# A graph kernel in fp32 on one core: the heads of two attention layers are set end to end

## The reference

```python
def gat_conv(x, src, dst, W, a_src, a_dst, bias, H, C, n):
    h = (x @ W).reshape(n, H, C)
    s_src = (h * a_src).sum(-1)
    s_dst = (h * a_dst).sum(-1)
    e = leaky_relu(s_src[src] + s_dst[dst], 0.2)
    ee = exp(e - segment_max(e, dst)[dst])
    alpha = ee / segment_sum(ee, dst)[dst]
    return segment_sum(alpha[:, :, None] * h[src], dst).reshape(n, H * C) + bias
out1 = gat_conv(layer_norm(x), ..., W1, a_src1, a_dst1, b1, 4, 192, N)
out2 = gat_conv(out1, ..., W2, a_src2, a_dst2, b2, 2, 96, N)
x = layernorm(x + concat([x, out2]) @ Wu + bu)
# then a relational graph layer: 34 relations, each a 768x768 weight, and a GCN
```

## Time and profile before

| | |
|---|---|
| median of 3 runs | 3441.8 us (3441.11 to 3443.11) |
| the profiled execution | 3440.49 us, of which the span is 3438.6 us |
| busy in the span | PE 93%, DVE 66%, ACT 42%, POOL 48% |
| gat1, first mask step to PE's end | from 554.58 us to 716.45 us |
| gat2, first mask step to PE's end | from 795.01 us to 859.94 us |
| one chunk of gat2 on PE, ten matmuls of 97 columns | 2.42 us |
| turning `out2` (L2101), start | 862.87 us, after an idle time of 2.94 us |
| the four weight maxima behind gat2's normalise (L1577) | 5.13 us from 862.85 us |
| loads of `xu_dram` behind gat2's normalise | 4.4 us from issue to landing |
| load of Wux issued, and PE's first work on x tiles (L1986) | 205.69 us and 453.23 us |
| weights of the first relation, issued | 784.91 us |

### The profile page before, as it was taken

How to read it: one execution, slowest core, us unless ns; L and a number is a source line. 1 busy time by engine, 2 the same in 40 slices (tenths; PEclk the granted TensorE clock), 3 DMA queues, 4 the chain that set the end, 5 groups by cost and what they waited for, 6 DMA issues and landing times. The chain is left out here.

```text
span 3438.6 us, 59477 instructions
## 1 busy us (share of the span) xinstructions
PE 3187.5 (93%) x17127; PEld 1997.9 (58%) x17127; DVE 2263.9 (66%) x4636; ACT 1452.8 (42%) x2678; POOL 1636.4 (48%) x1373
## 2 busy tenths in 40 slices
PE   6989988887589999999999999999999998879998
PEld 4544457886345555555555666666666664435545
DVE  8989997758844454554544878888888774533324
ACT  3767745636333333333343546555554632000100
POOL 3730000000346657666632665666666635777771
PEclk9999998998789999999999999999999999989999
DMA  3020012011243333333333555646555545675551
GB/s 97 2 74 0 0 54 82 1 45 43 94 123 109 126 126 109 126 117 119 126 108 131 178 185 174 203 160 199 177 181 178 175 148 158 185 227 157 159 128 52
DMA packets 230649, 415.83 MB, mean 121 GB/s; under 512 B 37108, under 2 KB 179955, under 8 KB 230566
## 3 DMA queue, kind: packets, MB, share of 16 engines
q1 hardware_dynamic: 169696, 272.25, 23.0%
q0 software_dynamic: 60480, 142.01, 15.5%
q10 hardware_dynamic: 390, 0.50, 0.1%
HBM read 263.22 MB, written 151.32 MB: 121 GB/s over the span
## 5 line engine op out<-in xcount | busy, mean ns | idle before, releaser
L2174 PE MATMUL bank<-arena 128*128 128x384 f16 x3675 | 1202.0, 327 | 22.0 <-DVE arena L1718 11.6
L2176 PE MATMUL bank<-arena 128*128 128x384 f16 x3675 | 1200.7, 327 | 0.0
L2177 PE MATMUL bank<-arena 128*128 128x384 f16 x3675 | 1200.5, 327 | 0.0
L1143 ACT ACTIVATE arena<-bank,winv 128x384 f32<-128x384 f32 x700 | 401.1, 578 | 878.4 <-PE bank L2177 861.8
L1718 DVE SCALAR_TENSOR_TENSOR arena<-bank,winv,arena 128x384 f32<-128x384 f32 x525 | 316.7, 613 | 412.5 <-PE bank L2177 411.4
L2174 PEld LDWEIGHTS bank<-arena 128*128 128x128 f16 x3675 | 360.1, 98 | 275.3 <-DVE arena L1718 17.2
L2177 PEld LDWEIGHTS bank<-arena 128*128 128x128 f16 x3675 | 360.1, 98 | 238.8 <-issue 2.0
L2176 PEld LDWEIGHTS bank<-arena 128*128 128x128 f16 x3675 | 360.5, 98 | 233.3 <-issue 6.5
L749 POOL DMA_INDIRECT arena<-y_half,idx_now x360 | 400.6, 1113 | 172.7 <-issue 101.8
L1611 DVE SCALAR_TENSOR_TENSOR arena<-arena,wscale 128x1152 f16<-128x1152 f32 x245 | 366.5, 1530 | 169.9 <-ACT arena L1054 162.0
L736 POOL DMA_INDIRECT w_now<-rel_inv_dram,idx_now x360 | 341.1, 947 | 253.9 <-ACT idx_now L1128 153.1
(11 more groups left out here) (245 smaller groups left out, 4136.3 us busy)
## 6 DMA issues: line engine op xcount, KB each, us to landing
y_half<-arena SPq DMA_DIRECT2D x306, 384.0 KB
arena<-in_L_gnn_W_rel_dram SPq DMA_DIRECT2D x68, 1152.0 KB, 5.9
arena<-y_half,idx_now POOLq DMA_INDIRECT x720, 3.2
y_half<-arena SPq DMA_DIRECT2D x34, 294.0 KB
w_now<-rel_inv_dram,idx_now POOLq DMA_INDIRECT x360, 2.6
cT_dram<-arena SPq DMA_DIRECT2D x1, 5625.0 KB
arena<-cT_dram SPq DMA_DIRECT2D x9, 625.0 KB
arena<-in_x_dram SPq DMA_DIRECT2D x10, 384.0 KB, 11.1
```

Source lines behind the costliest of these rows:

```text
L1143: nc.scalar.activation(y[half][:, :, c * CQ:(c + 1) * CQ], acc, ACT.Copy, scale=scale).then_inc(r_copied, 1)
L2174: nc.tensor.matmul(acc, h, w_hi[m - 1][:, k, :], start=fresh and k == 0, stop=False, skip_group_check=True)
L2176: nc.tensor.matmul(acc, h, w_lo[m - 1][:, k, :], start=False, stop=False, skip_group_check=True)
L2177: ins = nc.tensor.matmul(acc, l, w_hi[m - 1][:, k, :], start=False, stop=k == KH - 1, skip_group_check=True)
```

## The change

The change touches both attention layers and nothing else:

- Next head's rows: PE turns `zz` after chunk 1 and `lmax` after chunk 4. ScalarE copies `zz` after its Exp of chunk 4 into the other of two tiles (`bcL`, `unused`), and `lmax` into `bc1` after that of chunk 8. `leaky` and `minus` run one chunk ahead across the head boundary too.
- First head: its `zz` row goes to banks 2 to 4, right behind the `lmax` row, and VectorE copies it out. cT tile 8 is turned ahead of the rows, tile 9 behind them. A one-column Exp on ScalarE stands ahead of its row copy.
- Sums: PE's last chunk of a head signals after each bank, and normalise waits bank by bank. Its product is one broadcast multiplication per bank (and one more for the 98-row tile), without the bias.
- Biases: `b1` and `b2` are loaded as columns, element by element, and ScalarE adds them while it copies the turned `out1` and `out2`. The two loads that broadcast them to 128 partitions are gone.
- `out1` and `out2` are turned as soon as the banks that a group needs are normalised.
- The W2 step moves from behind gat1 into VectorE's program of heads 1 and 2, one pair in each of chunks 2 to 7.

```diff
-prod2 = unused[:, 0:D2]
+prod2 = view(vecV + 8 * D2, [D2])
...
-b2row = view(vecV + 8 * D2, [D2])
+b2col = bcol[:, 0:H2]
...
+  def summed(g, i):
+    h, c = divmod(i, NT)
+    return h * (NT - 1 + g.banks) + (NT - 1 + g.banks if c == NT - 1 else c + 1)
+  def bank_summed(g, h, k):
+    return h * (NT - 1 + g.banks) + NT + k
...
+O1_BANKS = (5, 6, 7, 0, 1, 2)
+def out_needed(g, k):
+  last = cdiv(NBANKS[g][1], P) - 1
+  here = O1_BANKS[k] + 1 if O1_BANKS[k] < gat1.banks else 0
+  return max(last // gat1.per + 1, here)
...
+gat2 = Gat("gat2", H2, C2, s2, s2_ready, h2, out2)
+O2_BANK = gat2.banks
...
-    ("x", range(4, 6)), ("row", 3), ("x", range(6, X_FIRST)), ("cT", range(CT_EARLY, CT_WAITS)),
-    ("row", H1), ("row", H1 + 1), ("cT", range(CT_WAITS, NT))]
+    ("x", range(4, 6)), ("row", 3), ("x", range(6, X_FIRST)), ("cT", range(CT_EARLY, NT - 1)),
+    ("row", H1), ("row", H1 + 1), ("cT", range(NT - 1, NT))]
+CT_LAST = (NT - 1) * len(NBANKS)
+def cT_bank(i):
+  return bank[i % 5 if i < CT_LAST else (0, 1, 5)[i - CT_LAST]]
...
-  sp.dma_start(row_a[:, :], b1.partition_broadcast(P)).then_inc(row_loaded, 16)
...
   sp.wait_ge(h_ready, NT * HALVES)
+  with nc.allow_non_contiguous_dma(reason="short vectors, a few hundred elements"):
+    sp.dma_start(gcol[:, :], col(b1)).then_inc(row_loaded, 16)
...
+  with nc.allow_non_contiguous_dma(reason="short vectors, a few hundred elements"):
+    sp.dma_start(b2col[0:C2, :], b2.rearrange("(j c) -> c j", c=C2)).then_inc(a2_loaded, 16)
   def keep_xu(n):
...
+        nc.scalar.copy(cT[0:rows(c), c, a:b], cT_bank(i)[0:rows(c), 0:b - a]).then_inc(cT_ready, 1)
...
-    else:
+    elif which == H1:
+      nc.scalar.activation(credit[:, 3:4], ones[:, 0:1], ACT.Exp)
       act.wait_ge(gat1.max, NT * H1)
-      spread_copy(gat1, which, (bc1, bcL)[which - H1])
+      spread_copy(gat1, H1, bc1)
...
-        act.wait_ge(g.pv, i - 3)
+        act.wait_ge(g.pv, g.summed(i - 4))
       nc.scalar.activation(ring[i % 4][0:r, :], bc1[0:r, :], ACT.Identity,
                 bias=mx[0:r, c, h:h + 1]).then_inc(g.lk, 1)
     if g is not gat1:
...
-      row(g.H + 1, bcL)
     act.wait_ge(g.shift, 2)
...
-      if c + 1 < NT:
+      if i + 1 < g.H * NT:
         leaky(i + 1)
       r = rows(c)
       act.wait_ge(g.t, i + 1)
       nc.scalar.activation(ring[i % 4][0:r, :], ring[i % 4][0:r, :], ACT.Exp).then_inc(g.ex, 1)
+      if h + 1 < g.H and c == 4:
+        row(g.H + 2 * h + 2, (bcL, unused)[(h + 1) % 2])
       if h + 1 < g.H and c == NT - 2:
         act.wait_ge(g.lk, NT * (h + 1))
-        row(g.H + 2 * h + 2, bc1)
-      if h + 1 < g.H and c == NT - 1:
-        leaky(i + 1)
-        act.wait_ge(g.t, NT * (h + 1))
-        row(g.H + 2 * h + 3, bcL)
+        row(g.H + 2 * h + 3, bc1)
   gat(gat1)
+  act.wait_ge(row_loaded, 16)
...
-      nc.scalar.copy(o1T[:, k, a:b], bank[i % 6][:, 0:b - a]).then_inc(o1T_ready, 1)
+      nc.scalar.activation(o1T[:, k, a:b], bank[O1_BANKS[k]][:, 0:b - a], ACT.Identity,
+                bias=gcol[:, k:k + 1]).then_inc(o1T_ready, 1)
   nc.scalar.copy(h2.rearrange("p n h c -> p (n h) c")[:, :, C2], ones[:, 0:NT * H2]).then_inc(h_ones, 1)
   for n in range(NT):
...
-      nc.scalar.copy(o2T[0:C2, j, a:b], bank[i][0:C2, 0:b - a]).then_inc(o2T_ready, 1)
+      nc.scalar.activation(o2T[0:C2, j, a:b], bank[O2_BANK + i][0:C2, 0:b - a], ACT.Identity,
+                bias=b2col[0:C2, j:j + 1]).then_inc(o2T_ready, 1)
...
-    dve.wait_ge(g.shift, 2)
+    dve.wait_ge(g.bc_psum, g.H + 2)
+    for j, (a, b) in enumerate(NBANKS):
+      ins = nc.vector.tensor_copy(bcL[:, a:b], bank[2 + j][:, 0:b - a])
+    ins.then_inc(g.shift, 1)
+    dve.wait_ge(g.shift, 3)
     def minus(i):
       h, c = divmod(i, NT)
       r = rows(c)
-      if c == 0:
-        dve.wait_ge(g.bc, g.H + 2 * h + 2)
+      if c == 0 and h:
+        dve.wait_ge(g.bc, g.H + 2 * h)
...
+      nc.vector.scalar_tensor_tensor(ring[i % 4][0:r, :], (bcL, unused)[h % 2][0:r, :], g.s[0:r, c, h:h + 1],
                      ring[i % 4][0:r, :], ALU.add, ALU.max).then_inc(g.t, 1)
     def normalise(h):
-      dve.wait_ge(g.pv, NT * (h + 1))
       for k in range(g.banks):
+        dve.wait_ge(g.pv, g.bank_summed(h, k))
...
+        at = slice(h * g.C, (h + 1) * g.C)
+        num = bank[k][:, 0:g.per * (g.C + 1)].rearrange("p (a c) -> p a c", c=g.C + 1)[:, 0:len(full), 0:g.C]
+        ins = nc.vector.tensor_tensor(
+          g.res[:, full[0]:full[-1] + 1, at], num,
+          rden[:, full[0]:full[-1] + 1].unsqueeze(2).broadcast_to([P, len(full), g.C]), ALU.mult)
         for b in tiles:
-          r = rows(b)
-          at = slice(h * g.C, (h + 1) * g.C)
-          ins = nc.vector.scalar_tensor_tensor(g.res[0:r, b, at], g.acc(b, r, 0, g.C), rden[0:r, b:b + 1],
-                            g.brow[0:r, at], ALU.mult, ALU.add)
+          if b not in full:
+            r = rows(b)
+            ins = nc.vector.tensor_scalar(g.res[0:r, b, at], g.acc(b, r, 0, g.C), rden[0:r, b:b + 1],
+                           None, ALU.mult)
         ins.then_inc(g.out, 1)
...
-      if (i + 1) % NT:
+      if i + 1 < g.H * NT:
         minus(i + 1)
...
-        minus(i + 1)
+      if g is gat1 and h in (1, 2) and 2 <= c < 2 + KT:
+        w2_vectors((h - 1) * KT + c - 2)
...
+  def w2_vectors(i):
+    k, j = divmod(i, 2)
+    if i == 0:
+      dve.wait_ge(w2_loaded, 16)
+      dve.wait_ge(a2_loaded, 48)
+    after(nc.vector.tensor_tensor(prod2, W2s[:, k, 0:D2], (a2s, a2d)[j], ALU.mult))
+    ins = nc.vector.tensor_reduce(W2s[:, k, D2 + j * H2:D2 + (j + 1) * H2],
+                   prod2.rearrange("p (h c) -> p h c", h=H2), AX.X, ALU.add)
+    after(ins)
+    if i == 2 * KT - 1:
+      nc.vector.memset(credit[:, 2:3], 0.0).then_inc(w2a_ready, 1)
   dve.wait_ge(mask_ready, NT)
...
   gat(gat1)
-  dve.wait_ge(w2_loaded, 16)
-  dve.wait_ge(a2_loaded, 48)
-  dve.wait_ge(gat1.pv, NT * H1)
-  for k in range(KT):
-    for j, a in enumerate((a2s, a2d)):
-      after(nc.vector.tensor_tensor(prod2, W2s[:, k, 0:D2], a, ALU.mult))
-      after(nc.vector.tensor_reduce(W2s[:, k, D2 + j * H2:D2 + (j + 1) * H2],
-                     prod2.rearrange("p (h c) -> p h c", h=H2), AX.X, ALU.add))
-  nc.vector.memset(credit[:, 2:3], 0.0).then_inc(w2a_ready, 1)
...
     if done == g.H:
       pe.wait_ge(g.shift, 1)
-    if done:
-      pe.wait_ge(g.bc, done)
+    if done == g.H + 1:
+      if g is gat1:
+        pe.wait_ge(cT_ready, CT_LAST)
+      else:
+        pe.wait_ge(xu_copied, HALVES * NT)
+    elif done:
+      pe.wait_ge(g.bc, done if done <= g.H else done - 1)
     g.turned[0] = done + 1
     h, k = divmod(done - g.H, 2)
-    column = g.s[:, :, done] if done < g.H else (lmax, zz)[k][:, :, h]
+    column = g.s[:, :, done] if done < g.H else ((zz, lmax) if h else (lmax, zz))[k][:, :, h]
+    first = 2 if done == g.H + 1 else 5
     for n in range(NT):
...
       at = n * P % BANK
-      ins = nc.tensor.transpose(bank[5 + n * P // BANK][:, at:at + r],
+      ins = nc.tensor.transpose(bank[first + n * P // BANK][:, at:at + r],
...
-        if i >= cs[0] * len(NBANKS) + 5:
+        if cs[0] * len(NBANKS) + 5 <= i < CT_LAST:
           pe.wait_ge(cT_ready, i - 4)
+        if i == CT_LAST + 2:
+          pe.wait_ge(gat1.bc, H1 + 1)
...
           r = rows(n)
-          ins = nc.tensor.transpose(bank[i % 5][0:rows(c), n * P - a:n * P - a + r],
+          ins = nc.tensor.transpose(cT_bank(i)[0:rows(c), n * P - a:n * P - a + r],
                        counts[0:r, n, c * P:c * P + rows(c)], ident[0:r, 0:r])
...
-    pe.wait_ge(cT_ready, len(NBANKS) * (cs[-1] + 1))
+    if cs[-1] != NT - 2:
+      pe.wait_ge(cT_ready, len(NBANKS) * (cs[-1] + 1))
...
           ins = nc.tensor.matmul(g.acc(b, r), ring[(h * NT + c) % 4][0:rc, b * P:b * P + r],
                      g.h[0:rc, c, h, :], start=(c == 0 and b % g.per == 0),
                      stop=(c == NT - 1), skip_group_check=True)
-        ins.then_inc(g.pv, 1)
-        if c in (NT - 3, NT - 2) and h + 1 < g.H:
+          if c == NT - 1 and (b % g.per == g.per - 1 or b == NT - 1):
+            ins.then_inc(g.pv, 1)
+        if c < NT - 1:
+          ins.then_inc(g.pv, 1)
+        if c in (1, 4) and h + 1 < g.H:
           row()
...
   for g, (a, b) in enumerate(NBANKS):
...
         pe.wait_ge(o1T_ready, i - 5)
+      pe.wait_ge(gat1.out, (H1 - 1) * gat1.banks + out_needed(g, k))
...
-        ins = nc.tensor.transpose(bank[i % 6][:, n * P - a:n * P - a + r], out1[0:r, n, k * P:(k + 1) * P],
+        ins = nc.tensor.transpose(bank[O1_BANKS[k]][:, n * P - a:n * P - a + r], out1[0:r, n, k * P:(k + 1) * P],
...
-  pe.wait_ge(gat2.out, H2 * gat2.banks)
-  pe.wait_ge(gat2.bc, 3 * H2)
+  pe.wait_ge(gat2.bc, 3 * H2 - 1)
...
+      pe.wait_ge(gat2.out, j * gat2.banks + (cdiv(b, P) - 1) // gat2.per + 1)
...
-        ins = nc.tensor.transpose(bank[i][0:C2, n * P - a:n * P - a + r], out2[0:r, n, j * C2:(j + 1) * C2],
```

(1 more changed line is left out.)

16 lines of the change are left out of this document (6 added, 10 removed).

## The result

The changed kernel takes 3405.68 us (median of 4 runs, 3403.84 to 3407.63); the kernel before, in the same comparison, 3442.45 (4 runs, 3441.11 to 3444.12). The ratio is 0.9895, interval 0.9883 to 0.9906: 36.8 us less, where 40.2 were predicted. The profiled execution took 3403.84 us (span 3402.0, mean clock 0.977), 36.65 less than that of before, and is used for the sum.

The account below looks back on a forecast made before the run. PE was taken to set the pace inside a head, with time lost at head boundaries and layer starts and ends. Six terms summed to 40.2 us, 3440.5 to 3400.3, given as 3401.5 for the median; range 3394 to 3413.

Parts of the forecast that it names:

- A: Start of gat1: first mask step at 549.15 instead of 554.58, 5.4 us gained, bounds 4 and 6.5.
- B: gat1's three head boundaries: VectorE's 2.2 us lead and normalise of 3.6 us gain 16.1 us, bounds 11 and 19.
- C: From gat1 to h2: turning takes 9.7 us with ScalarE's 18 copies as chain, 4.5 us gained, bounds 3 and 6.
- D: Start of gat2: first mask step at 791.45 instead of 795.01, 3.5 us gained, bounds 2.5 and 4.5.
- E: Inside gat2, bound by VectorE: mask steps run 56.5 us instead of 61.7, 5.2 us gained, bounds 3.5 and 5.5.
- F: End of gat2: PE's end to first addition takes 7.2 us instead of 12.7, 5.5 gained, bounds 2.5 and 6.
- Rival 1: Heads 1 and 2 of gat1: VectorE becomes the bound through chunks with W2 pairs; 3408, chance 0.11.
- Rival 2: Ahead of x tile 3: the element load of b2 delays it by up to 6.5 us; 3408, chance 0.05.
- Rival 3: Boundaries, C and F: TensorE's clock falls after remaining waits, 2 to 2.6 us each; 3412, chance 0.06.
- The stretch behind it should keep its length: Behind the first addition, expected near 832.5 after gat2: the changed profile would show no change in length.
- Rival 4: gat1's chunks: the clock stays low through them, 2.6 us a chunk, slower than before, up to 3505; chance 0.03.
- Rival 5: Behind 872.65: an unmoved transfer or weight load makes something wait and gives the gain back; 3441, chance 0.03.

Follow-up runs that it names:

- e5: The changed kernel itself, unchanged, run again; 3405.06 us beside 3443.21 for the kernel before, ratio 0.9889.
- e12: The changed kernel itself, unchanged, run a third time; 3583.69 us beside 3621.14 for the kernel before, ratio 0.9894.
- e2: The changed kernel, but normalise waits ahead of every bank for the signal of the head's last bank; 3600.48 us, ratio 0.9930 to the kernel before.
- e3: The changed kernel with the division tile by tile, ten products for a head instead of one for each bank; 3672.48 us, ratio 1.0124 to the kernel before.
- e8: The changed kernel with late rows (turned at chunks 7 and 8, lmax first) and the old boundary order; 3425.51 us, ratio 0.9945 to the kernel before.
- e9: The changed kernel with late rows alone (turned at chunks 7 and 8), new boundary order kept; 3618.45 us, ratio 0.9988 to the kernel before.
- e1: The changed kernel with the next head's first leaky and minus back behind the last chunk's Exp and mask step; 3587.43 us, ratio 0.9891.
- e4: The changed kernel with W2's twelve pairs back behind gat1's last normalise; 3587.95 us, ratio 0.9895 to the kernel before.
- e7: The changed kernel with every second of the 18 copies of turned features done by VectorE instead of ScalarE; 3401.36 us, ratio 0.9879.
- e10: The changed kernel with copies of turned features shared by ScalarE and VectorE, unread transposes in TensorE's waits, column products with a scalar operand; 3578.07 us, ratio 0.9876.
- e6: The changed kernel with TensorE's short waits filled by transposes that nobody reads; 3401.86 us beside 3405.06 for the changed kernel.
- e11: The changed kernel with the division tile by tile, the same kernel as e3 run once more; 3663.54 us, ratio 1.0122 to the kernel before.

## Why the prediction held, and where it was off

In us, by the prediction's own terms, from the table (after, with e5 and e12 in brackets):

| term | predicted | measured |
|---|---|---|
| A, start of gat1 | 5.4 | 5.55 (4.49, 4.04) |
| B, boundaries | 16.1 | 16.27 (15.70, 15.95) |
| C, gat1 to h2 | 4.5 | 4.54 (4.55, 4.53) |
| h2 product | none | -1.68 (-0.02, -1.69) |
| D, to gat2 | 3.5 | 2.14 (3.58, 3.57) |
| E, inside gat2 | 5.2 | 5.99 (5.86, 5.35) |
| F, to the first addition | 5.5 | 6.14 (6.14, 5.28) |
| to the relations | none | -1.88 (-1.93, -0.05) |
| behind them | none | -0.47 |
| sum | 40.2 | 36.6 |

The six terms with a mechanism sum to 40.6, in e5 and e12 to 40.3 and 38.7. That the first is within 0.5 of 40.2 is luck in part: D fell short by 1.4, E and F went over by 0.8 and 0.6. The rest of the loss is in stretches that the prediction left as they were. (The last step of the sum, 3400.3 and 1.3, gives 3401.6 and not 3401.5.)

- A and D were right in their steps: the copy of `zz` by VectorE, the table load ahead. From the start of the `lmax` row to gat1's first mask step are 14.55 us before, 8.91 after and in e12, and 9.63 in e5, so 5.6, 5.6 and 4.9; the rest of the difference in the table lies ahead of that row, which starts between 539.7 and 542.4 in these profiles. D's 2.14 comes from both spread rows at 1.2 GHz; the other two profiles have 3.58 and 3.57.
- B rested on VectorE's lead of 2.2 us and a normalise of 3.6. e2 measured the lead as a wait of 2.2; normalise took 3.64 in the changed kernel, and e3 shows that its length passes through. From TensorE's end of head 0 (587.90) to its end of gat1 (694.63) are 106.7 us, as predicted; 0.2 of the table's 16.27 lie in head 0. What the prediction had not separated is which part carries the gain: it takes the early place of the rows (e8, e9) and, with it, normalise by signals (e2), while undoing the order alone costs nothing (e1), where I expected 1.5 us a boundary. Rival 1 is refuted by e4.
- C: 9.7 predicted for the turning, 9.67 measured, with ScalarE as the chain; e7 shows the chain by removing it.
- E: the sum took 19 intervals of 2.80 between mask steps. The last two mask steps stand directly behind each other, before (853.83) as after (2.85 us for both), so the last interval is 1.4; small waits gave back 0.6. First to last mask step took 55.7 where 56.5 were predicted.
- F: it was added up over TensorE's product (7.2, between 6.7 and 8.2). Measured were 6.57, set by VectorE's weight maxima, which the prediction had ending at 6.6 and left out of the sum. In e12, with the product at the lower level, TensorE decides: 7.43.
- Rival 2 did not happen: TensorE waits less ahead of x tile 3 than the 5.65 us of the earlier trace rows:

```profile
482.26 1.51 PE L2029 MATMUL bank<-ident,arena 128*128 128x128 f32 x6 [4.25 <-issue]
```

- Rival 3 put the falls of the clock behind the boundaries. In gat1 there were none behind waits of 1.05 to 1.24 us. But behind gat2's boundary, with a wait of 1.27 us, the chunks stood at the lower level in e4, e7, e10 and e12 and not in the changed kernel's first profile, e2, e5 and e6, and the clock fell in the h2 product, behind 1.6 us. "The stretch behind it should keep its length" and the h2 product taken at its old length are the steps that failed: in eight of the nine profiles in which TensorE turned as in the change (e4 among them, with a wait of 2.6), h2 took 21.7 to 23.1; in e5 20.28; in the three where TensorE's wait was filled or shorter (e6, e7, e10), 20.24 to 20.28, and 20.28 in e2, where the turning starts later and the wait of 1.6 us is there too. So a wait of this kind was followed by the fall in most profiles, not in all, and its removal by none. The load beside it (377 GB/s in the 5 us above) does not explain it. In e5 it ran beside a product at full clock (167 GB/s on the mean of the stretch), and in the kernel before too (171):

```profile
730.66:750.92 20.26, 20.26 (x120) 19.91 (x120) 0.00 (x0) 3.52 (x19) 0.00 (x0) 1.00 0.48 171
```

- Rival 4 did not happen: from 562.05 on gat1 ran at 1.00 in every stretch shown above.
- Rival 5 is true in small, though not by a transfer. Of the 1.88 lost on the way to the relations, 0.8 is VectorE's wait for GpSimd (interval between the first two additions 6.47 for 5.67) and 1.1 a product at 1.2 GHz (the second 5.41 for 4.34). The first arose because the first addition came earlier relative to GpSimd's sums, so that F's larger gain of 6.14 paid for it; in e12 the addition came 0.86 later, and it was not lost. The second is the clock's: e4, e7, e8 and e9, with the addition as early, have 4.34.

What stays open: the 0.47 at the end, which is within what this stretch varies (2491.0 to 2493.9 at the lower level of the relation layers); why the relation layers take 175 us more in two comparisons; and the extra 65 to 81 us of e3 and e11.

## What to carry to other kernels

Ask of a stage boundary which input of the next stage comes last, and compute that one ahead: here early rows are worth 15 us, and the same new order with late rows lost 10. Undo parts one by one and together: the signals by bank were worth 8 us of gat1 with early rows, and with late rows all that was kept of the change gained 0.4. A sum of terms, each read from rows, came within 1.4 us of each term measured and, partly by errors that cancelled, within 0.5 us of their sum in the first profile; what it missed stood in the stretches taken as unchanged, where an earlier arrival met another engine's work and where a short wait lowered the clock. Compare by stages, in more than one profile of the same kernel, when the differences are under 5 us.

## What the runs showed of the hardware

- **TensorE's clock amplifies short waits, and not each time.** The same kernel had its h2 product at 21.94, 20.28 and 21.95 us. A wait of 1.6 us stood ahead of it in all three, and in two the clock fell about 1 us into the product (at 705.2 and 707.3) and stood at 1.2 GHz for a stretch that cost 1.7 us. Ahead of the wait TensorE had turned pieces with waits of 0.16 us between them.
- **Transposes alone held the upper level.** In e10, 5.7 us of nothing but transposes stood at 1.00, and the first chunks behind ran at 1.00, where the kernel without them had 0.61. In the changed kernel TensorE ran nothing but transposes from 531.48 to 544.04, too (100 of them, 11.64 us busy), at 1.00. The Trainium skill ("TensorE: Matmul & The Clock Gate", Part 4: PE-mode transpose) says that transposes do not count as the array's activity in the same way; by that rule the filling would have done nothing. The measurement differs, and it decides here.
- **A VectorE operation with two tile operands in SBUF waited for GpSimd's end,** however small: 128x1 took 0.98 us instead of 0.16 and ended 0.02 behind GpSimd's, and so in nine more profiles. With one tile and one scalar operand it took 0.21 beside the same GpSimd operation (e10). The Trainium skill ("SBUF — State Buffer", SBUF: two separate sides) tells of a shared pair of ports that belongs, for a whole instruction, to whichever of a VectorE operation with two inputs in SBUF and a GpSimd operation starts first; the trace agrees.
